# A decoder's first attention: slot scores and slot sums from rounded parts

## The reference

```python
s = hs @ Ws1.T @ Ws2.T + bs2                # Ws1 (16, 256), Ws2 (1024, 16)
s = jnp.clip(s, -CLAMP, CLAMP).reshape(B, T, H, M).transpose(0, 2, 1, 3)
z = jax.lax.cumlogsumexp(s, axis=2)
es = jnp.exp(s)
enz = jnp.exp(-z)
A = jnp.where(mask, jnp.einsum('bhtd,bhjd->bhtj', q, k) * scale, 0.0)
ok = enz * jnp.einsum('bhtj,bhjm->bhtm', A, es)
qv = jax.nn.softmax(ok, axis=-1)
W2 = jnp.where(mask, jnp.einsum('bhtm,bhjm->bhtj', qv * enz, es), 0.0)
o = jnp.einsum('bhtj,bhjd->bhtd', W2, v)
```

## Time and profile before

| | us |
|---|---|
| median of 3 runs (1756.58 to 1759.71) | 1758.63 |
| the profiled execution | 1762.23 |
| its span | 1760.4 |
| TensorE busy | 1624.6 |
| VectorE busy | 1283.4 |
| ScalarE busy | 840.4 |
| GpSimd busy | 554.6 |

### The profile page before, as it was taken

One profiled execution on the slowest core, in us unless ns is written; L12 is line 12 of the kernel. 1 busy time (PEld: TensorE's weight loads), 2 busy tenths in 40 slices (PEclk: granted clock), 3 DMA queues, 4 the chain that ended last, 5 costly groups with the idle time before them and its releaser, 6 DMA issues.

```text
span 1760.4 us, 51382 instructions
## 1 busy us (share of the span) xinstructions
PE 1624.6 (92%) x21686; PEld 1145.0 (65%) x21686; DVE 1283.4 (73%) x2850; ACT 840.4 (48%) x1372; POOL 554.6 (32%) x949
## 2 busy tenths in 40 slices
PE   6999999999958899998999888998998899999989
PEld 5899999999743455554566555665454466666657
DVE  8877787788586888878898352443467798988954
ACT  3433433433441566556567712442243376776752
POOL 5454544534251222403302031541112123431230
PEclk9999999999988999999999979999999999999999
DMA  4010100110026553352462383562913036764200
GB/s 132 1 49 1 49 13 15 65 33 1 21 74 115 101 140 59 100 102 38 102 122 50 72 325 121 190 206 106 163 37 66 20 65 133 133 106 77 42 2 25
DMA packets 91856, 143.93 MB, mean 82 GB/s; under 512 B 14870, under 2 KB 60123, under 8 KB 91628
## 3 DMA queue, kind: packets, MB, share of 16 engines
q1 hardware_dynamic: 87228, 127.79, 31.6%
q10 hardware_dynamic: 2528, 7.74, 1.3%
q0 software_dynamic: 1872, 5.13, 0.8%
HBM read 109.68 MB, written 32.03 MB: 81 GB/s over the span
## 4 chain that ended last, share of the span: by engine, by line
PE 75%; DVE 14%; issue 4%; ACT 4%; POOL 1%; DMA 1%; another core or an unknown queue 1%; ACTq 0%; SPq 0%; POOLq 0%; DVEq 0%
PE bank L1002 22%; PE bank L1210 8%; PE bank L1959 5%; PE bank L1845 4%; PE bank L1847 4%; PE bank L1846 4%; PE bank L740 3%; PE bank L1978 3%; DVE xa_part_max L1283 3%; PE bank L2406 2%; PE bank L677 2%; DVE shared L1283 2%; PE bank L2421 1%; ACT xa_e L1244 1%; PE bank L704 1%
## 5 line engine op out<-in xcount | busy, mean ns | idle before, releaser
L1283 DVE TENSOR_REDUCE xa_part_max<-bank 128x1 f32<-128x448 f32 (+1 forms) x512 | 266.3, 568 | 22.3 <-PE bank L1002 19.5
L1244 ACT ACTIVATE xa_e<-bank 128x1024 f32<-128x1024 f32 (+1 forms) x208 | 211.7, 1023 | 107.5 <-PE bank L1002 105.9
L1244 ACT ACTIVATE ca_e<-bank 128x1024 f32<-128x1024 f32 (+2 forms) x208 | 197.8, 958 | 75.5 <-PE bank L1002 74.5
L1283 DVE TENSOR_REDUCE shared<-bank 128x1 f32<-128x400 f32 (+1 forms) x384 | 205.5, 570 | 21.3 <-PE bank L1002 18.0
L1002 PE MATMUL bank<-xa_kst,xa_qst 122*32 122x448 bf16 (+1 forms) x2048 | 177.5, 345 | 16.1 <-DVE xa_part_max L1283 7.7
L1210 PE MATMUL bank<-xa_e,xa_vaug 128*17 128x256 f32 (+1 forms) x1664 | 132.2, 383 | 4.7 <-ACT xa_e L1244 2.5
L1002 PE MATMUL bank<-xa_qst,xa_kst 128*32 128x256 bf16 (+1 forms) x3264 | 134.1, 274 | 0.0
L1210 PE MATMUL bank<-ca_e,ca_vaug 128*17 128x256 f32 (+2 forms) x1664 | 124.1, 365 | 7.0 <-issue 4.5
L938 POOL TENSOR_TENSOR gsa_qk<-gsa_qk,gsa_rot 128x512 f32<-128x512 f32 x64 | 81.8, 1278 | 138.1 <-DVE gsa_rot L856 138.1
L1002 PE MATMUL bank<-xa_wkv,shared 128*32 128x256 f32 (+1 forms) x1632 | 111.1, 393 | 5.6 <-DVE xa_r L1659 2.5
L1002 PEld LDWEIGHTS bank<-xa_qst,xa_kst 128*32 128x32 bf16 (+1 forms) x3264 | 92.9, 97 | 30.5 <-issue 3.0
(11 more groups left out here) (406 smaller groups left out, 4149.2 us busy)
## 6 DMA issues: line engine op xcount, KB each, us to landing
xa_kst<-xa_k_parts SPq DMA_DIRECT2D x96, 200.1 KB, 5.6
ca_kst<-ca_k_parts SPq DMA_DIRECT2D x96, 200.1 KB, 5.2
xa_k_parts<-xa_parts SPq DMA_DIRECT2D x24, 400.2 KB, 4.8
ca_k_parts<-moe_ctx_parts SPq DMA_DIRECT2D x8, 1200.8 KB
moe_gu<-in_expert_gate_up SPq DMA_DIRECT2D x8, 1024.0 KB
shared<-in_ctxT_split ACTq DMA_DIRECT2D x4, 1601.0 KB, 9.2
moe_ctxT<-in_ctxT SPq DMA_DIRECT2D x8, 800.5 KB, 8.0
ca_cv<-in_ctx SPq DMA_DIRECT2D x4, 1536.0 KB
```

What stands on the lines that cost most here:

```text
L1244: e.activation(self.e[m % 3][0:rows, :, first:T], banks[m % 2][0:rows].rearrange("p a (h t) -> p (a h) t", t=T)[:, :, first:T], ACT.Exp, s ...
L1283: e.tensor_reduce(top, work[:, 0:hi - lo], AX.X, ALU.max).then_inc(*reduced(t, *step))
```

## The change

**Scores.** The partitions from 0, from 32 and from 64 now hold parts. The `u` step's product is formed three times, into partitions 0, 32 and 64 of its bank; ScalarE writes the rounded part of rows 0 to 15 and 64 to 79 into `u`, and of rows 32 to 47 into a scratch tile; VectorE writes the rest into rows 32 to 47 of `u`. `ws2` holds the rounded part in rows 0 to 16 and 32 to 48 and the rest in rows 64 to 80 (three loads in place of one, two ScalarE casts and a VectorE subtraction, once). The `es` product is then one rounded matmul over 96 rows for each 256 columns.

**Sums.** ScalarE takes the exponential twice: first rounded, into the new tile `es_hi`, then in place. GpSimd subtracts the two into the new tile `es_rest`. The `cs` step is six rounded matmuls, on `es_hi` and `es_rest`, in place of three plain ones. There is one `es_hi` and one `es_rest`, so ScalarE's part of `es` n, and GpSimd's, wait for the matmuls of `cs` n-1. In the written order `cs` 1 therefore moves up to stand before `es` 2, and `cs` 2 before `es` 3.

The diff, without the tile list and the masks' setup:

```diff
                     ("qk", 3), ("w_split", 0, "g"), ("qk", 4), ("norm_turn", 0, 5), ("ok", 0), ("h_split", 2), ("a", 2), ("norm", 0, 6), ("qk", 5), ("ok", 1), ("u", 2),
                     ("cs", 0), ("a", 3), ("norm_turn", 0, 6), ("v", 0, 0), ("qk", 6), ("ok", 2), ("es", 1), ("a", 4), ("norm", 0, 7), ("et", 0), ("sm_max", 0),
-                    ("ok", 3), ("a", 5), ("es", 2), ("qk", 7), ("gate", 0), ("ok", 4), ("et", 1), ("qk", 8), ("sm_exp", 0), ("v", 0, 1), ("ok", 5), ("a", 6), ("et", 2),
-                    ("a", 7), ("cs", 1), ("v", 1, 0), ("qk", 9), ("v", 1, 1), ("z", 0), ("gate", 1), ("ok", 6), ("z", 1), ("norm_turn", 0, 7), ("ok", 7),
-                    ("sm_max", 1), ("w2", 0), ("qk", 10), ("a", 8), ("sm_exp", 1), ("a", 9), ("qk", 11), ("u", 3), ("o", 0), ("es", 3), ("cs", 2),
+                    ("ok", 3), ("a", 5), ("cs", 1), ("es", 2), ("qk", 7), ("gate", 0), ("ok", 4), ("et", 1), ("qk", 8), ("sm_exp", 0), ("v", 0, 1), ("ok", 5), ("a", 6), ("et", 2),
+                    ("a", 7), ("v", 1, 0), ("qk", 9), ("v", 1, 1), ("z", 0), ("gate", 1), ("ok", 6), ("z", 1), ("norm_turn", 0, 7), ("ok", 7),
+                    ("sm_max", 1), ("w2", 0), ("qk", 10), ("a", 8), ("sm_exp", 1), ("a", 9), ("qk", 11), ("u", 3), ("o", 0), ("cs", 2), ("es", 3),
                     ("w2", 1), ("a", 10), ("ok", 8), ("o", 1), ("rr", 0), ("v", 2, 0), ("cs", 3), ("wo_scale", 0), ("h_split", 3), ("gate", 2), ("scale", 0, 0),
                     ("gate", 3), ("scale", 0, 1), ("a", 11), ("z", 2), ("ok", 9), ("w_split", 1, "q"), ("ok", 10), ("w2", 2), ("z", 3),
...
                     m.then_inc(*u_mm(n))
                 elif kind == "es":
                     g, b = divmod(n, B)
                     q.wait_ge(u_ready, "u", b)
-                    q.wait_ge(gsa_in["ws2"], "gsa")
+                    q.wait_ge(ws2_lo, "ws2")
+                    q.wait_ge(ws2_hi, "ws2")
                     for i in range(TB):
-                        m = e.matmul(ps[:, i * GM:(i + 1) * GM], u[b][:, i * P:(i + 1) * P], ws2[:, g * GM:(g + 1) * GM], start=True, stop=True)
+                        m = e.matmul(ps[:, i * GM:(i + 1) * GM], u[b][0:U_ROWS, i * P:(i + 1) * P].bitcast(F32R), ws2[0:U_ROWS, g * GM:(g + 1) * GM].bitcast(F32R),
+                                     start=True, stop=True)
                     m.then_inc(*es_mm(n))
                 elif kind == "cs":
-                    eb = es[n % 2]
-                    q.wait_ge(es_ready, n)
-                    q.wait_ge(gsa_in["causal"], "gsa")
-                    e.matmul(ps[:, 0:GM], causal[:, 0:P], eb[:, 0, :], start=True, stop=True)
-                    e.matmul(ps[:, GM:2 * GM], ones, eb[:, 0, :], start=True, stop=False)
-                    e.matmul(ps[:, GM:2 * GM], causal[:, 0:P], eb[:, 1, :], start=False, stop=True).then_inc(*cs_mm(n))
+                    parts = [es_hi[:].bitcast(F32R), es_rest[:].bitcast(F32R)]
+                    c_, o_ = causal[:, 0:P].bitcast(F32R), ones.bitcast(F32R)
+                    q.wait_ge(es_rested, n)
+                    for i, p in enumerate(parts):
+                        e.matmul(ps[:, 0:GM], c_, p[:, 0, :], start=(i == 0), stop=(i == 1))
+                    for i, p in enumerate(parts):
+                        e.matmul(ps[:, GM:2 * GM], o_, p[:, 0, :], start=(i == 0), stop=False)
+                        m = e.matmul(ps[:, GM:2 * GM], c_, p[:, 1, :], start=False, stop=(i == 1))
+                    m.then_inc(*cs_mm(n))
                 elif kind == "et":
                     q.wait_ge(es_ready, n)
...
+                        q.wait_ge(gsa_in["ws2"], "gsa")
+                        e.copy(ws2_top[64:U_ROWS, :].bitcast(F32R), ws2_raw[64:U_ROWS, :])
+                        e.copy(ws2[0:64, :].bitcast(F32R), ws2_raw[0:64, :]).then_inc(*ws2_hi("ws2"))
+                    else:
+                        q.wait_ge(u_ready, "u", n - 1)
                     q.wait_ge(u_mm, n)
-                    e.copy(u[n][0:RANK, :], home(kind, j)[0:RANK, 0:T]).then_inc(*u_ready(*step))
+                    for r, to in zip(U_PARTS, (u[n], u_top, u[n])):
+                        m = e.copy(to[r:r + RANK, :].bitcast(F32R), home(kind, j)[r:r + RANK, 0:T])
+                    m.then_inc(*u_hi(n))
                 elif kind == "h_split":
...
                     q.wait_ge(clipped, *step)
+                    if n:
+                        q.wait_ge(cs_mm, n - 1)
+                    else:
+                        q.wait_ge(gsa_in["causal"], "gsa")
+                        e.copy(causal[:].bitcast(F32R), shared[:, 4 * D:4 * D + 2 * P])
+                    e.activation(es_hi[:].bitcast(F32R), es[n % 2][:], ACT.Exp)
                     e.activation(es[n % 2][:], es[n % 2][:], ACT.Exp).then_inc(*es_ready(n))
...
-                if kind == "es":
+                if kind == "u":
+                    if n == 0:
+                        q.wait_ge(ws2_hi, "ws2")
+                        e.tensor_tensor(ws2[64:U_ROWS, :].bitcast(F32R), ws2_raw[64:U_ROWS, :], ws2_top[64:U_ROWS, :], ALU.subtract).then_inc(*ws2_lo("ws2"))
+                    r = U_PARTS[1]
+                    q.wait_ge(u_hi, n)
+                    e.tensor_tensor(u[n][r:r + RANK, :].bitcast(F32R), home(kind, j)[r:r + RANK, 0:T], u_top[r:r + RANK, :], ALU.subtract).then_inc(*u_ready(*step))
+                elif kind == "es":
                     if n >= 2:
                         q.wait_ge(ok_mm, G4 * (n - 1) - 1)
...
                     seen(aT[n % 2]).then_inc(*a_ready(n))
+                elif kind == "es":
+                    q.wait_ge(es_ready, n)
+                    if n:
+                        q.wait_ge(cs_mm, n - 1)
+                    e.tensor_tensor(es_rest[:].bitcast(F32R), es[n % 2][:], es_hi[:], ALU.subtract).then_inc(*es_rested(n))
                 elif kind == "sm_exp":
                     q.wait_ge(sm_sum, n)
                     e.tensor_tensor(sm[n % 2][:], sm[n % 2][:], enz[n % 3][:], ALU.mult).then_inc(*sm_ready(n))
```

More of the change, by code:

```diff
@@ L439, in build @@
         mx, ssum, ss = sb("mx", [P, TB, G4]), [sb(f"ssum{i}", [P, TB, G4]) for i in range(2)], [sb(f"ss{i}", [P, TB, G4]) for i in range(2)]
-        qz_all = sb("qz", [P, 4, T])
-        qz = [qz_all[:, i] for i in range(2)]
+        qz = [sb(f"qz{i}", [P, T])[:] for i in range(2)]
+        es_hi = sb("es_hi", [P, TB, GM])
         tg = [sb(f"tg{i}", [P, BANK]) for i in range(2)]
@@ L447, in build @@
         ogT = [sb(f"ogT{i}", [P, G4, P]) for i in range(TB)]
+        es_rest = sb("es_rest", [P, TB, GM])
         gsa.close()
+        U_PARTS, U_ROWS = (0, 32, 64), 96
+        ws2_raw, u_blank, u_top, ws2_top = (shared[0:U_ROWS, f:f + w] for f, w in ((0, HEADS * SLOTS), (5 * T, T), (6 * T, T), (8 * T, HEADS * SLOTS)))
+        u_hi, ws2_hi, ws2_lo = (local("gsa", n) for n in ("u_hi", "ws2_hi", "ws2_lo"))
+        es_rested = local("gsa", "es_rest")
         gsa_in = {k: landing(f"gsa_{k}") for k in ("ws1", "ws2", "rope", "causal", "gw")}
@@ L600, in gsa_loads @@
             q.wait_ge(zeroed, "ws2")
-            e.dma_start(ws2[0:RANK + 1, :], a["Ws2T"]).then_inc(*gsa_in["ws2"]("gsa", by=16))
+            for r in U_PARTS:
+                e.dma_start(ws2_raw[r:r + RANK + 1, :], a["Ws2T"]).then_inc(*gsa_in["ws2"]("gsa", by=16))
             e.dma_start(cos[:], const("cos")).then_inc(*gsa_in["rope"]("gsa", by=16))
             e.dma_start(sin[:], const("sin")).then_inc(*gsa_in["rope"]("gsa", by=16))
-            e.dma_start(causal[:], const("causal")[:, 0:2 * P]).then_inc(*gsa_in["causal"]("gsa", by=16))
+            e.dma_start(shared[:, 4 * D:4 * D + 2 * P], const("causal")[:, 0:2 * P]).then_inc(*gsa_in["causal"]("gsa", by=16))
             load_wo(0)
@@ L635, in gsa_pe @@
                     for c in range(DC):
-                        m = e.matmul(ps[0:RANK, 0:T], ws1[:, c, :], hT[:, c, n * T:(n + 1) * T], start=(c == 0), stop=(c == DC - 1))
+                        for r in U_PARTS:
+                            m = e.matmul(ps[r:r + RANK, 0:T], ws1[:, c, :], hT[:, c, n * T:(n + 1) * T], start=(c == 0), stop=(c == DC - 1), skip_group_check=True)
                     m.then_inc(*u_mm(n))
@@ L913, in seen @@
                 return e.affine_select(part, part, [[0, 2], [1, P]], ALU.is_ge, 0.0, base=0, channel_multiplier=-1)
-            e.memset(ws2[:], 0.0).then_inc(*zeroed("ws2"))
+            e.memset(ws2_raw, 0.0).then_inc(*zeroed("ws2"))
+            e.memset(u_blank, 0.0).then_inc(*pool_own())
+            q.wait_ge(pool_own)
+            for r in U_PARTS[::2]:
+                e.memset(u_blank[r:r + 32, :], 1.0).then_inc(*pool_own())
+            q.wait_ge(pool_own)
             for t in u:
-                e.memset(t[:], 0.0).then_inc(*pool_own())
-                q.wait_ge(pool_own)
-                e.memset(t[0:32, :], 1.0).then_inc(*zeroed("u"))
+                e.tensor_copy(t[0:U_ROWS, :].bitcast(F32R), u_blank).then_inc(*zeroed("u"))
             for step, places in gsa_order:
```

## The result

The changed kernel takes 1784.37 us (median of 4 runs, 1779.31 to 1788.26); the kernel before takes 1758.80 beside it. The ratio is 1.0148, with a 95% interval of 1.0121 to 1.0175: **slower by 26 us**, where 13 were forecast, and just outside the range (to 1783). The profiled executions are 1788.26 us (span 1786.5) and 1762.23 (span 1760.4): 26.1 us apart.

What follows compares the result with a forecast made beforehand. TensorE's queue was taken as the bound. Start +2.1, units 1 and 3 +4.1 each, clock +3.3, turns +2.4, -2.7, -1.0, turn 15 +1.6 were summed to +13.8 us: median 1758.6 becomes 1772, range 1757 to 1783.

Steps and rivals of the forecast that it cites:

- stops: Units 1 and 3: TensorE waits for subtraction and reciprocal, then for a mask queued behind a subtraction; +4.1 us each.
- turns: Turns 4 to 14: subtraction delays GpSimd's scaling; +2.4 us over seven split turns, -2.7 over three unsplit, -1.0 for turn 14.
- the clock: TensorE's granted clock falls behind both waits at units 1 and 3, losing 1.66 us each; +3.3 us.
- The two casts and the added loads end while ScalarE has nothing to do: Start: casts and loads hidden in ScalarE's 8.1 us gap before 20.95; only VectorE's added subtractions cost, +2.1 us.
- rival 1: Whole kernel: all added work is covered, 19.4 us saved in full less 2.1 at the start, 1741; chance 0.08.
- its term: `es` step on TensorE: two rounded matmuls (0.24 us) in place of four instructions (0.86) save 0.62 us per unit.
- Turn 15: Last turn: subtraction comes behind GpSimd's scaling, `cs` 15 starts 2.2 us later and is 0.59 shorter; +1.6 us.
- Rival 3: More lost: `u` in line 2 us for two sequences, port wait 2.2, split turns 0.3 more; about +9, 1781; chance 0.15.
- rival 4: `es` step: 96-row matmul no faster than plain, 0.38 us more, +2 at most, 1774; chance within the forecast's 0.60.
- What follows turn 15 moves as a whole: Program behind turn 15: hangs on the same chain and shifts as a whole, with no term of its own.

Runs made afterwards that it cites:

- e3: Changed kernel with a second pair of buffers for units 1 and 3 and the old order of `cs` 1 and `cs` 2: ratio to before 1.0100.
- r8: Changed kernel with the split of a weight moved from the middle of a turn to its end: ratio to before 1.0092.
- r7: Only the scores half of the change, sums as in the kernel before: ratio to before 1.0014.
- r10: Changed kernel with each 17-row load of the slot weights cut into 16 rows and 1: ratio to before 1.0164.
- f2: Repeat of the changed kernel with slot-weight loads cut into 16 rows and 1, beside the unaltered changed kernel: ratio to before 1.0139, 1781.6 us.
- r11: Scores half only, with loads of 16 and 1 rows, casts behind the `u` 0 copies, subtraction moved to `h_split` 1: ratio to before 0.9989.
- r5: Changed kernel with the two WoT loads issued behind the first two weight reloads: ratio to before 1.0153.
- r6: Changed kernel with WoT loads later, cos and sin loads first, casts behind the `u` 0 copies, slot-weight subtraction at `u` 1: ratio to before 1.0128.
- f1: The changed kernel itself, unaltered, measured again: ratio to before 1.0169, median 1790.0 us.
- e1: Changed kernel with the three slot-weight loads issued ahead of the two big weight loads: ratio to before 1.0168.
- e2: Changed kernel with the slot weights' casts and subtraction moved from `u` 0 to `u` 1: ratio to before 1.0166.
- e4: Changed kernel with GpSimd's subtraction of a unit behind the turn's second scaling and the sum matmuls one step later: ratio to before 1.0131.
- r12: Only the sums half of the change, one buffer and moved order, scores as in the kernel before: ratio to before 1.0094.
- f4: Sums half only, with second buffers, unit 3's subtraction later, weight splits at turn's end, last sum one step later: ratio 0.9973, 1753.2 us.

## Why the prediction was wrong

- **The direction, and the mechanisms of stops and turns: right.** Slower, by waits in queue order. The single buffer makes the stops (e3), the split ahead of the subtraction the longer turns (r8), and both belong to the sums (r7).
- **Stops: right in place and size.** With the clock, twice 4.1 + 1.66 = 11.5 us forecast, 6.5 + 6.2 = 12.7 measured. Of it the clock has 2.4 and 1.7 by the windows above, for 1.66 each, which leaves 4.1 and 4.5 for the waits, for 4.1 each.
- **The step that failed: "The two casts and the added loads end while ScalarE has nothing to do".** The term was +2.1 and is +8.4. ScalarE's gap was real, but the loads filled it. In the kernel before, `ws2` is first used at 25.97 us; the change moved that use to the cast at 12.7 and tripled the load, and I priced neither the landing nor its shape, only the casts behind it. Measured, the cast begins at 20.08, after a wait of 7.40 us for the load, and the normalization comes 5.6 us late. The trace of before bounds the landing only by 25.97, and that should have been said. r10 and f2 give the rest: with the landing repaired the normalization is 2.0 and 1.66 us late, for 1.65. `es` 0 is still 3.5 us late in r10 and 3.3 in f2; the 1.2 to 1.4 us beyond the term go with TensorE's pause at 24 us (3.07 us in r10, 2.95 in f2) and a clock of 0.91 behind it, which I infer from their place and did not test alone. r11, which takes the subtraction off this path as well, has `es` 0 at 27.9.
- **The clock was forecast for the two stops only.** It was also down in 20 to 40 us (0.74; 1.00 before) and in turn 4. That turn took 31.0 us in five of the eleven profiles with rounded sums that split a weight ahead of the scaling (changed, e3, r5, r6, f1) and 29.0 to 29.4 us in the other six (e1, e2, e4, r10, r12, f2). What decides it is open; the change's profile has the longer one.
- **Turns: right by two errors.** Split turns of 29.0 and unsplit ones of 27.8 us were forecast exactly. But the saving is 0.9 us per unit, not 1.2 (0.3 for `es`, 0.6 for `cs`), the wait is 1.1 (1.5 in turn 4), not 1.6, and in unsplit turns there is none, not 0.3. The errors cancel here. Where the waits are gone they would not: 16 x 0.9 is 14 us, so rival 1's 1741 was out of reach.
- **Why `es` saves half of its term**: at the step itself the 0.62 us are there. From the `qk` products ahead of it to the second matmul behind it, before takes 1.20 us (169.89 to 171.09) and the changed kernel 0.58 (192.06 to 192.64). But what follows is slower: the four transposes of `z` take 0.59 us from start to next start where they took 0.44, before and then changed:

```profile
172.41 0.60 PE L695 MATMUL bank<-ident,gsa_sm 128*128 128x128 f32 x4
172.85 0.33 PE L688 MATMUL bank<-gsa_es,gsa_aT 128*128 128x64 f32 x2
```
```profile
193.95 0.60 PE L707 MATMUL bank<-ident,gsa_sm 128*128 128x128 f32 x4
194.54 0.44 PE L700 MATMUL bank<-gsa_es,gsa_aT 128*128 128x64 f32 x2
```

  It goes with the rounded `es`: r12 and f4, whose `es` is plain, have 0.44, r7 and r8 0.57 to 0.62. In r7 the `ok` matmuls behind lose another 0.1. What slows them I don't know.
- **Turn 15**: `cs` 15 starts 2.1 us later, 2.2 forecast.
- **Rival 3's 1781 lies nearest, by other causes.** `u` is not in line (1.05 us for 1.04 at full clock), a split turn grows by 0.3 as forecast, and the normalization of 2.57 us takes 0.42 in the changed kernel. Its own terms also add up to 8.3, not 9, and rival 4's 0.38 does not follow from its rows; neither bears on the miss.
- **"What follows turn 15 moves as a whole"**: not quite. The same code behind 557 us of before takes from 1.8 us less to 12.4 us more than in before's profile, over all profiles but that of f4 (11.3 less). Before's own medians differ by 6.6 us between the chips. So one pair of profiles places a loss within the slot stage, but not a few us of the total. In r10's profile this part has the 12.4, enough to hide its gain in the first ratio; where it comes from is open.

Of the 12.3 us that separate 13.8 from 26.1, then: start 6.3, turns 2.3 (the clock in turn 4 above all), stops 1.2, from `cs` 15 on 2.9, less 0.6 between these; the 0.1 that is left is rounding in the forecast's sum, whose terms as written give 13.9.
